# Adapter matmuls of a four-layer attention kernel in fp16 halves, transposed by DMA, and their layer-norm steps ahead of the score maxima

## The chip, the cores and the metric

The kernel runs on one core of a Trainium2 chip. The metric is the device time of one execution in microseconds, the median of three runs.

## The reference, cut to what matters

Eight batches, each with `x` and `f` of 512 tokens by 512. Four residual layers follow one another:

```python
x = x + L0(x, f)                       # 16-head attention, keys from x (masked by length) and one own key from f; then Wo
q = x + embed[stage]                   # L1
x = x + softmax(q @ f.T) @ f
h = relu(x @ W1[lang] + b1[lang])      # L2, the adapter: W1 512x128, W2 128x512
y = x + h @ W2[lang] + b2[lang]
x = x + layernorm(y) * gamma[lang] + beta[lang]
t = x @ lora_A[rl].T                   # L3, rank 16
x = x + t @ lora_B[rl].T + lang_embed[rl]
```

The change concerns L2 and L3. `lang` and `rl` are chosen per batch, so their weights are loaded for each batch.

## The kernel before, in words

All matrices of 128 partitions are handled by tiles of 128 tokens; a batch has four (`NT`), and 512 columns are four blocks of 128 (`ND`). Large products are made in fp16 with each operand as a high and a low half, by three matmuls a pair (`hi_lo`, L478): high by high, low by high, high by low. Halves are made by GpSimd (`split`, L513 and L515), by ScalarE and VectorE together, or by VectorE. Matrices `xT` and `fT` (tokens along the free axis) come from `split16` by a transposing DMA on SyncE's queue (`turn`, L698).

The program is unrolled over batches. Each engine runs the same list of steps in its own order: attention of batch i (scores, ScalarE's exponentials, values), then `layer1` (Wo and L1), then `mid`. `mid` is made of three interleaved things:

- the projections of the next batch i+1: `K`, `Q`, `KS`, `VS`, `V`, each cut into six parts of two matmuls. The prediction calls one such part a slot; there are 117 of them, numbered from 0, K of group 0 having 0 to 5, Q 6 to 11, KS 12 to 17, and so on by 18 for a group;
- 64 steps `SMAX` of the next batch (the maxima): TensorE makes a 128x512 score tile (L1378), VectorE takes its row maximum (L1095), ScalarE the exponential with its sum (L816). Two pairs of banks (4 and 6) hold four such tiles at a time. One `SMAX` follows each slot, in four groups of 16 that open at slots 35, 53, 71 and 89. `SMAX` of group g needs `KQ`, filled by 12 DMAs (L645) from the halves that GpSimd makes of Q and K (`HALF`);
- the adapter steps (L2 and L3) of batch i, one after every other slot, from the list `adapters` of `order_mid`. All use bank 2 on TensorE.

For one tile of 128 tokens the adapter steps before are: `X2T` (TensorE transposes x in fp32, L1280; ScalarE evicts it to `x2T`, L833; GpSimd adds b2, L550), `HID` (four fp32 matmuls of 128 columns, L1406; ScalarE relu, L839), `ADP` (one fp32 matmul of 512 columns, L1411; VectorE adds and sums, L1141), `SQ` (ScalarE, L845), `NORM` (for two tiles at a time: 15 small VectorE instructions in five pieces, L1035 to L1048, then two L1053; GpSimd adds beta, L556), `SCALE` (GpSimd times gamma, L560, and add, L563), `X3T` (fp32 transposes; VectorE copies, L1152), `LOW` (four fp32 matmuls with the rank-16 rows; ScalarE, L851), `LORA` (fp32 matmul of 512 columns, L1433; VectorE adds, L1156; SyncE stores).

After the last `SMAX` come `MROW` and `SROW`, which turn maxima and sums into the shift rows and normalisers that attention of the next batch needs. Batch 0 has a `mid` without adapters, and the last batch has the adapters without projections (`order_last`).

In attention, VectorE makes four copies of lora_B (L1193), and TensorE transposes the small tables (`small_tables`); ScalarE evicts them (L871).

## Times and profile before

| | us |
|---|---|
| median of 3 runs | 1296.07 (1295.64 to 1298.99) |
| the profiled execution | 1295.73 |
| its span | 1294.0 |
| TensorE busy | 1257.0 (97%) |
| VectorE busy | 864.2 (67%) |
| ScalarE busy | 847.8 (66%) |
| GpSimd busy | 490.0 (38%) |
| share of the last chain: TensorE, VectorE, ScalarE | 69%, 15%, 12% |

From the second batch on the kernel repeats with a period of 156.10 us: layer 1 of a batch, its `mid`, attention of the next. The period shown below begins at 598.80 us; the first row of the windows is its layer 1, the next three are `mid` (to the opening of the maxima, the maxima, the rest), the fifth is attention. A matmul's record lasts longer than the distance to the next, since matmuls overlap; what one costs TensorE's queue is read from the chain, whose pieces do not overlap.

### The profile page before, as it was taken

What the parts mean: (1) busy time and instruction counts of PE and PEld (TensorE: products, weight loads), DVE (VectorE), ACT (ScalarE), POOL (GpSimd) and SP (SyncE); (2) the same over time, 40 slices, a digit from 0 to 9 for tenths busy, and PEclk for the clock granted to TensorE, in tenths of its full rate; (3) what the DMA queues carried; (4) which work ended last, traced back from release to release, by engine and by line L of the source; (5) the groups of instructions that cost most, each with busy time, mean ns of one, the idle gap of its engine ahead of it and who ended that gap; (6) DMA issues with size and microseconds to landing.
All of it is one profiled execution on the core that took longest, in us unless ns stands there. A gap on an engine that the chain in (4) does not pass through costs nothing.

```text
span 1294.0 us, 19231 instructions
## 1 busy us (share of the span) xinstructions
PE 1257.0 (97%) x6697; PEld 523.5 (40%) x6697; DVE 864.2 (67%) x1561; ACT 847.8 (66%) x1795; POOL 490.0 (38%) x428
## 2 busy tenths in 40 slices
...
GB/s 217 83 6 107 124 57 66 79 80 99 52 63 122 37 98 68 47 125 63 86 58 50 117 79 77 58 50 108 98 75 66 46 95 124 50 66 90 4 33 33
DMA packets 156142, 98.85 MB, mean 76 GB/s; under 512 B 107338, under 2 KB 130182, under 8 KB 156046
## 3 DMA queue, kind: packets, MB, share of 16 engines
...
## 4 chain that ended last, share of the span: by engine, by line
PE 69%; DVE 15%; ACT 12%; issue 2%; POOL 1%; DMA 1%; SPq 0%; ACTq 0%; POOLq 0%; DVEq 0%
PE bank L478 25%; PE banks L478 13%; PE banks L1443 8%; DVE nmx L1095 8%; PE bank L1459 7%; ACT banks L816 5%; PE banks L1378 4%; ACT big L867 4%; PE bank L1280 3%; PE bank L1406 2%; PE bank L1411 2%; PE bank L1433 2%; PE bank L1469 1%; DVE y L1053 1%; ACT bank L896 1%
## 5 line engine op out<-in xcount | busy, mean ns | idle before, releaser
L816 ACT ACTIVATE banks<-banks,nmx 128x512 f32<-128x512 f32 x512 | 341.2, 682 | 40.2 <-DVE nmx L1095 37.8
L1095 DVE TENSOR_REDUCE nmx<-banks 128x1 f32<-128x512 f32 x512 | 329.2, 687 | 19.5 <-PE banks L1378 18.6
L867 ACT ACTIVATE big<-banks 128x1024 f32<-128x1024 f32 x256 | 248.0, 1021 | 54.4 <-PE banks L1443 53.4
L478 PE MATMUL bank<-fT,w_hi 128*128 128x512 f16 x768 | 255.7, 379 | 0.6 <-DVE fT L1009 0.6
L1378 PE MATMUL banks<-KQ 97*128 97x512 f16 x512 | 195.6, 382 | 8.1 <-ACT banks L816 7.9
L513 POOL TENSOR_TENSOR split<-tiles_in,ones 128x512 f16<-128x512 f32 x56 | 62.0, 1108 | 224.7 <-DMA xT<-split 205.7
L1443 PE MATMUL banks<-KQ 98*128 98x512 f16 x512 | 143.5, 383 | 3.6 <-DVE q L1116 0.2
L478 PE MATMUL bank<-fT,w_lo 128*128 128x512 f16 x384 | 145.4, 379 | 0.0
L513 POOL TENSOR_TENSOR half<-qk,ones 128x512 f16<-128x512 f32 x64 | 68.4, 1069 | 200.6 <-ACT qk L798 192.5
L1459 PE MATMUL bank<-big,V 128*32 128x512 f32 x1024 | 136.4, 605 | 0.0
L588 POOL TENSOR_TENSOR x<-x,bo_rows 128x512 f32<-128x512 f32 x32 | 39.9, 1275 | 206.5 <-DMA x<-in_x_dram 206.5
L816 ACT ACTIVATION_READ_ACCUMULATOR banks<-banks,nmx 128x1 f32 x512 | 116.5, 227 | 0.0
L478 PEld LDWEIGHTS bank<-fT,w_hi 128*128 128x128 f16 x768 | 75.1, 98 | 82.0 <-issue 12.8
L1378 PEld LDWEIGHTS banks<-KQ 97*128 97x128 f16 x512 | 49.1, 96 | 104.5 <-ACT banks L816 56.9
L478 PE MATMUL bank<-fT,q1T 128*128 128x512 f16 x384 | 88.2, 379 | 1.8 <-DVE q1T L1213 1.8
L1443 PEld LDWEIGHTS banks<-KQ 98*128 98x128 f16 x512 | 34.2, 97 | 129.3 <-ACT big L867 100.0
L478 PE MATMUL bank<-xT,w_hi 128*128 128x512 f16 x256 | 84.3, 381 | 0.5 <-ACT qk L798 0.5
L478 PE MATMUL banks<-split,p_both 128*128 128x512 f16 x384 | 84.5, 379 | 0.0
L478 PE MATMUL bank<-w_hi,xT 128*128 128x512 f16 x256 | 81.5, 379 | 0.0
L560 POOL TENSOR_TENSOR y<-y,gr 128x512 f32<-128x512 f32 x32 | 42.8, 1337 | 92.5 <-DVE y L1053 92.5
L515 POOL TENSOR_TENSOR half<-qk,half 128x512 f16<-128x512 f32 x64 | 75.5, 1179 | 5.0
L478 PE MATMUL banks<-w_hi,xT 128*128 128x512 f16 x256 | 76.3, 380 | 0.0
(154 smaller groups left out, 1822.0 us busy)
## 6 DMA issues: line engine op xcount, KB each, us to landing
...
```

The lines of the kernel that those rows point to most:

```text
L478: mm = eng.matmul(out_ap, pairs[n][0], pairs[n][1], start=(first and n == 0), stop=(last and n == len(pairs) - 1))
L513: eng.tensor_tensor(high, src, ones[:, 0:1].to_broadcast([P, S]), ALU.mult).then_inc(high_done, 1)
L515: eng.tensor_tensor(low, src, high, ALU.subtract).then_inc(low_done, 1)
L560: eng.tensor_tensor(y[:, t % 2, :], y[:, t % 2, :], gr[:, :], ALU.mult).then_inc(scaled, 1)
L588: eng.tensor_tensor(x1[:, t, :], x1[:, t, :], bo_rows[:, :], ALU.add).then_inc(x_bo, 1)
L816: eng.activation(bank(step, i)[:, v, :], bank(step, i)[:, v, :], ACT.Exp, bias=nmx[:, t, h:h + 1], accum_out=esum[:, t, h:h + 1]).then_inc ...
L867: eng.activation(big[:, n % 2, 2 * u:2 * u + 2, :], bank(step)[:, :, :], ACT.Exp).then_inc(read(step), 1)
L1095: eng.tensor_reduce(nmx[:, t, h:h + 1], bank(step, i)[:, v, :], AX_X, ALU.max, negate=True).then_inc(max_done, 1)
L1280: mm = eng.transpose(tile_of(step, b)[:, d * P:(d + 1) * P], src[:, d * P:(d + 1) * P], ident[:, :])
L1378: eng.matmul(bank(step, i)[:, v, :], KQ[0:SHIFT_ROW, j, g, 1, t * P:(t + 1) * P], KQ[0:SHIFT_ROW, j, g, 0, :], start=True, stop=True).then ...
L1443: mm = eng.matmul(bank(step)[:, j % 2, :], KQ[0:SHIFT_ROW + 1, j, g, 0, k * P:(k + 1) * P], KQ[0:SHIFT_ROW + 1, j, g, 1, :], start=True, s ...
L1459: mm = eng.matmul(bank(("PV", g))[q, :], V[:, k, g * P + j * DH:g * P + (j + 1) * DH], big[:, n % 2, j, :], start=(k == 0), stop=(k == NT ...
```

## The change: what it does

- `X2T` and `X3T` leave TensorE for the seven batches with a next one. x2 is split into halves by ScalarE (`X2`) and VectorE (within `PV1` of layer 1), x3 by GpSimd (`X3`); both are transposed by DMA into `aT2` (L736, four turns each, `T3` for x3). The first f turn now stands ahead of the last p1 turn in SyncE's queue, the other three behind it.
- `HID` and `LOW` work on 256 tokens (two steps instead of four) with fp16 halves: 12 matmuls and 8 matmuls of 256 columns. `LORA` is one fp16 matmul; `ADP` stays fp32. W1 is loaded into `hT` and split by GpSimd (three instructions a batch). VectorE makes the low rows of `LOW`.
- `NORM` is once for all four tiles, 11 small instructions instead of twice 15. `U` (centre, times gamma) and `SCALE` (times the inverse deviation, plus x) are one VectorE instruction each for a tile; GpSimd's two of `SCALE` go, and `L1053` too.
- `HID` to `SCALE` stand ahead of slot 35, where the maxima open; `X3` to `LORA` in the slots up to 74.
- lora_B is copied by one instruction, the small tables are evicted mostly by VectorE, and lang_embed comes by its own small DMA into `erow`. Two `memset` more at the start. The last batch keeps its transposes on TensorE, and splits what they give.

```diff
-        adapters = [("X2T", 0), None, ("HID", 0), None, ("ADP", 0), None, ("X2T", 1), ("SQ", 0), ("HID", 1), ("ADP", 1),
-                    ("SQ", 1), n0[0], ("X2T", 2), n0[1], ("HID", 2), n0[2], ("X2T", 3), n0[3], ("HID", 3), n0[4],
-                    n0[5], None, ("SCALE", 0), None, ("SCALE", 1), ("X3T", 0), None, ("LOW", 0), None, ("ADP", 2),
...
+        at = {3: [("HID", 0)], 5: [("ADP", 0)], 6: [("ADP", 1), ("SQ", 0), ("HID", 1)], 7: [("SQ", 1)], 8: [("U", 0), ("ADP", 2)],
+              9: [("ADP", 3), ("SQ", 2), ("U", 1)], 10: [("SQ", 3), ("U", 2)], 11: [("NORM", 0), ("U", 3)],
+              12: [("SCALE", 0), ("SCALE", 1)], 13: [("SCALE", 2), ("SCALE", 3)], 16: [("X3", 0)], 17: [("X3", 1)],
+              18: [("X3", 2)], 19: [("X3", 3), ("T3", 0), ("T3", 1)], 20: [("T3", 2), ("T3", 3)],
+              28: [("LOW", 0)], 30: [("LORA", 0)], 32: [("LORA", 1)], 33: [("LOW", 1)], 35: [("LORA", 2)], 37: [("LORA", 3)]}
...
-    out, later = [], {}
+    out, later = [("X2", t) for t in range(NT) if tail], {}
...
# GpSimd
+                        if head:
+                            eng.wait_ge(f_lo, (i + 1) * NT + t + 1)
                         wait_read(eng, ("PV1", t), i)
-                        eng.tensor_tensor(xb[:, t % 2, :], x1[:, t, :], b2r[:, :], ALU.add).then_inc(xb_done, 1)
+                        eng.tensor_tensor(yb[:, t, :], x1[:, t, :], b2r[:, :], ALU.add).then_inc(xb_done, 1)
+                        if head and t == NT - 1:
+                            add_beta(range(NT), head, i)
+                    elif step[0] == "X3":
+                        eng.wait_ge(x3_done, i * NT + t + 1)
+                        eng.wait_ge(x2t_in[t // 2], i * 32 + 32)
+                        split(p16[:, t, 0:S], p16[:, t, S:2 * S], x1[:, t, :], x3_hi, i * NT + t + 1, x3_lo)
-                        eng.tensor_tensor(y[:, t % 2, :], y[:, t % 2, :], gr[:, :], ALU.mult).then_inc(scaled, 1)
...
-                        eng.tensor_tensor(x1[:, t, :], y[:, t % 2, :], x1[:, t, :], ALU.add).then_inc(x3_done, 1)
+            def split_w1(i):
+                eng.wait_ge(w1_in, i * 16 + 16)
+                eng.tensor_tensor(hT[:, :], hT[:, :], wide[:, 0:1].to_broadcast([P, S]), ALU.mult).then_inc(w1_wide, 1)
+                eng.wait_ge(w1_wide, i + 1)
+                halves = w1[:].rearrange("p h d n -> p h (d n)")
+                split(halves[:, 0], halves[:, 1], hT[:, :], w1_hi, i + 1, w1_lo)
# SyncE
                 for t in range(NT):
+                    if head and t == NT - 1:
+                        wait_full(eng, ("S1", NT - 1), i)
+                        turn_f(0, b)
...
+                    for n in range(1, NT):
+                        turn_f(n, b)
+                    for t in range(NT):
+                        eng.wait_ge(x2_lo, i * NT + t + 1)
+                        turn(aT2, t, p16[:, t, :], x2t_in[t // 2])
# ScalarE
+                    elif kind == "X2":
+                        wait_read(eng, ("PV1", t), i)
+                        eng.activation(p16[:, t, 0:S], x1[:, t, :], ACT.Copy).then_inc(x2_hi, 1)
# VectorE
+                        if head:
+                            eng.wait_ge(x2_hi, i * NT + t + 1)
+                            eng.scalar_tensor_tensor(out=p16[:, t, S:2 * S], in0=x1[:, t, :], scalar=1.0, in1=p16[:, t, 0:S],
+                                                     op0=ALU.mult, op1=ALU.subtract).then_inc(x2_lo, 1)
+            def centre(t, i):
+                eng.wait_ge(sq_done, i * NT + t + 1)
+                eng.scalar_tensor_tensor(out=yb[:, t, :], in0=yb[:, t, :], scalar=st[:, t, 1:2], in1=gr[:, :],
+                                         op0=ALU.add, op1=ALU.mult).then_inc(normed, 1)
+            def scale(t, head, i):
+                eng.wait_ge(newton, (i + 1 if head else i + 1 + t // 2) * NEWTON)
...
+                eng.scalar_tensor_tensor(out=x1[:, t, :], in0=yb[:, t, :], scalar=st[:, t, 4:5], in1=x1[:, t, :],
+                                         op0=ALU.mult, op1=ALU.add).then_inc(x3_done, 1)
# TensorE
+                        if head:
+                            eng.wait_ge(x2t_in[step[1]], i * 32 + 32)
...
+                        hi_lo(eng, bank(step, i)[:, 0:at.stop - at.start], [(w1[:, 0, d, :], w1[:, 1, d, :]) for d in range(ND)],
+                              [(aT2[:, 0, d, at], aT2[:, 1, d, at]) for d in range(ND)]).then_inc(done(step, i), 1)
...
+                        for d in range(ND):
+                            for h in range(2):
+                                rows = a16[:, h, d, :, :].rearrange("p c r -> p (c r)")
+                                mm = eng.matmul(bank(step, i)[0:3 * LR, 0:at.stop - at.start], rows, aT2[:, h, d, at],
+                                                start=(d == h == 0), stop=(d == ND - 1 and h == 1))
```

On VectorE, around the opening of the maxima, the program before has small statistics instructions (L1044 and its like) between `KS` products (L1084) and the first maxima (L1095):

```order
L1042 TENSOR_TENSOR st<-st 128x2
L1084 SCALAR_TENSOR_TENSOR prod<-bank,bias_ks,qk 128x512
L1095 TENSOR_REDUCE nmx<-banks 128x1 x4
L1044 TENSOR_TENSOR st<-st 128x2
L1046 TENSOR_SCALAR st<-st 128x2
L1048 TENSOR_TENSOR st<-st 128x2
L1095 TENSOR_REDUCE nmx<-banks 128x1 x2
L1053 TENSOR_SCALAR y<-y,st 128x512 x2
L1095 TENSOR_REDUCE nmx<-banks 128x1 x10
```

In the changed program the same place reads as follows (L1092 is the last of the small instructions, L1097 is `U`, L1104 `SCALE`, L1135 the product, L1146 the maxima):

```order
L1190 SCALAR_TENSOR_TENSOR tiles_in,st<-bank,tiles_in 128x512
L1194 TENSOR_SCALAR st<-st 128x1
L1097 SCALAR_TENSOR_TENSOR tiles_in<-tiles_in,st,gr 128x512 x2
L1083 TENSOR_SCALAR st<-st 128x4
...
L1092 SCALAR_TENSOR_TENSOR st<-st 128x4
L1097 SCALAR_TENSOR_TENSOR tiles_in<-tiles_in,st,gr 128x512
L1104 SCALAR_TENSOR_TENSOR x<-tiles_in,st,x 128x512 x4
L1135 SCALAR_TENSOR_TENSOR prod<-bank,bias_ks,qk 128x512
L1146 TENSOR_REDUCE nmx<-banks 128x1 x16
```

The whole of the statistics, with four `SCALE`, now stands in front of the first maximum, and the 16 maxima of a group are together.

On TensorE the place from the start of `mid` reads before, with transposes (L1280), `HID` (L1406) and `ADP` (L1411):

```order
L1280 MATMUL bank<-ident,x 128x128 x4
L478 MATMUL bank<-xT,w_hi 128x512 x2
...
L1406 MATMUL bank<-big,w 128x128 x4
L478 MATMUL bank<-xT,w_lo 128x512
...
L1411 MATMUL bank<-w,hT 128x512
```

and after the change (L504 with `big,w` is `HID`, L1503 `ADP`):

```order
L504 MATMUL bank<-big,w 128x256 x12
...
L1503 MATMUL bank<-w,hT 128x512
L504 MATMUL bank<-fT,w_lo 128x512
L504 MATMUL bank<-fT,w_hi 128x512 x2
L504 MATMUL bank<-fT,w_lo 128x512
L1503 MATMUL bank<-w,hT 128x512
L504 MATMUL bank<-big,w 128x256 x12
```

The second `HID` stands right behind the second `ADP`, in the same bank.

On SyncE's queue the part from the xT turns to the mask row was:

```order
L698 DMA_TRANSPOSE xT<-split 128x8x128 x4
L712 DMA_TRANSPOSE p_both<-big 128x8x128 x4
L698 DMA_TRANSPOSE fT<-split 128x8x128 x4
L636 DMA KQ<-mask_rows 1x16x512
L645 DMA KQ<-half 32x2x512 x4
```

and is now, with the four turns of x2 behind those of f:

```order
L736 DMA_TRANSPOSE xT<-split 128x8x128 x4
L756 DMA_TRANSPOSE p_both<-big 128x8x128 x3
L736 DMA_TRANSPOSE fT<-split 128x8x128
L756 DMA_TRANSPOSE p_both<-big 128x8x128
L736 DMA_TRANSPOSE fT<-split 128x8x128 x3
L736 DMA_TRANSPOSE big<-big 128x8x128 x4
L674 DMA KQ<-mask_rows 1x16x512
L683 DMA KQ<-half 32x2x512 x4
```

## Rows read from the trace of the kernel before

**Rows 1.** Windows: length, busy of PE, PEld, DVE, ACT, POOL; clock, DMA, GB/s

```profile
598.80:630.20 31.40, 31.18 (x154) 15.04 (x153) 16.12 (x31) 10.04 (x20) 9.88 (x9) 1.00 0.63 124
630.20:652.10 21.90, 21.90 (x124) 12.54 (x123) 7.91 (x20) 7.75 (x15) 13.86 (x13) 1.00 0.23 49
652.10:708.40 56.30, 55.52 (x289) 24.08 (x287) 51.83 (x102) 51.16 (x146) 22.49 (x19) 1.00 0.23 56
708.40:715.40 7.00, 7.00 (x41) 3.37 (x41) 4.41 (x8) 3.73 (x8) 0.00 (x0) 1.00 0.11 37
715.40:754.90 39.50, 39.13 (x226) 9.31 (x224) 25.52 (x29) 31.68 (x34) 14.69 (x12) 1.00 0.31 91
...
1223.20:1294.00 70.80, 55.76 (x265) 29.18 (x263) 32.74 (x86) 18.34 (x40) 20.49 (x16) 0.83 0.13 30
```

**Rows 2.** Chain that ended last, from 637 us: start, length, engine, tile, line

```profile
638.00 0.44 PE bank L1280 x4
638.43 1.73 PE bank L478 x8
640.16 0.89 PE bank L1406 x8
...
667.04 0.35 PE bank L1424 x8
...
670.11 0.86 PE bank L1411 x2
...
677.48 0.86 PE bank L1433 x2
```

**Rows 3.** ScalarE's exponentials in `mid`: source line in batch 0, then the period

```profile
L816 ACT ACTIVATE banks<-banks,nmx x64: 650/728/925, 37.6 to 85.1; 128x512 f32<-128x512 f32 x64
...
L816 ACT ACTIVATE banks<-banks,nmx x64: 650/664/738, 653.7 to 708.7; 128x512 f32<-128x512 f32 x64
```

**Rows 4.** TensorE timeline: first score matmuls of attention, steady, then batch 0

```profile
715.28 1.03 PE L1443 MATMUL banks<-KQ 98*128 98x512 f16 x4
717.44 1.13 PE L1443 MATMUL banks<-KQ 98*128 98x512 f16 x4
...
92.10 1.03 PE L1443 MATMUL banks<-KQ 98*128 98x512 f16 x4
```

**Rows 5.** Groups by line, 630 to 716 us: evictions

```profile
L798 ACT ACTIVATE qk<-bank,bias_k 128x512 f32<-128x512 f32 x4 | 2.8, 695 | 0.4 <-PE bank L478 0.4
...
L851 ACT ACTIVATE lowT<-bank,ident 128x128 f32<-128x128 f32 x4 | 1.5, 372 | 0.2 <-PE bank L1424 0.2
```

**Rows 6.** Timeline of VectorE and GpSimd where both work from SBUF

```profile
569.17 5.01 POOL L588 TENSOR_TENSOR x<-x,bo_rows 128x512 f32<-128x512 f32 x4 [24.47 <-DMA x<-in_x_dram]
...
569.57 3.43 DVE L1193 COPY smallb<-smallb 128x64 f32<-128x64 f32 x4 [3.52 <-DMA smallb<-in_L_cond_lora_B_dram]
...
645.59 0.17 DVE L1046 TENSOR_SCALAR st<-st 128x2 f32<-128x2 f32 x1
645.79 1.00 DVE L1048 TENSOR_TENSOR st<-st 128x2 f32<-128x2 f32 x1
...
649.49 0.16 DVE L1042 TENSOR_TENSOR st<-st 128x2 f32<-128x2 f32 x1
...
645.73 1.04 POOL L513 TENSOR_TENSOR half<-qk,ones 128x512 f16<-128x512 f32 x1 [1.42 <-ACT qk L798]
```

**Rows 7.** VectorE's two-input instruction from SBUF: source line, whole run

```profile
L1180 DVE SCALAR_TENSOR_TENSOR xT<-y,cols,xT x32: 750/752/1603, 110.1 to 1225.3; 128x512 f16<-128x512 f32 x32
```

**Rows 8.** SyncE's queue: issue times by source, landing time by issue group

```profile
L698 SPq DMA_TRANSPOSE fT<-split x4: 1323/1332/1337, 624.7 to 628.8; - x4
...
fT<-split SPq DMA_TRANSPOSE x28, 3.3
```

**Rows 9.** Timeline of the last batch's end, GpSimd

```profile
1279.34 1.50 POOL L560 TENSOR_TENSOR y<-y,gr 128x512 f32<-128x512 f32 x1 [5.91 <-DVE y L1053]
1280.91 1.26 POOL L563 TENSOR_TENSOR x<-y,x 128x512 f32<-128x512 f32 x1
```

More of the change, by code:

```diff
@@ L122, in order_mid @@
         if adapters and i % 2 == 0:
-            out += [a for a in (adapters.pop(0),) if a]
+            out += adapters.pop(0)
         if rows and not sums and i >= late and not adapters:
@@ L134, in order_mid @@
     assert rows and i >= max(later)
-    return out + [a for a in adapters if a] + ([] if sums else [("SROW",)])
+    return out + [a for each in adapters for a in each] + ([] if sums else [("SROW",)])
 OPEN = ((32, 26, 26, 26), (24, 24, 24, 24))
@@ L598, in _ @@
             add_bo(B - 1)
-            mid(True, False, B - 1, [step for step in order_last() if step in ADAPTER_STEPS])
+            split_w1(B - 1)
+            mid(True, False, B - 1, [step for step in order_last() if step[0] in ADAPTERS])
         @block.sync
```

353 lines of the change are left out of this document (198 added, 155 removed).

## The prediction, made before the changed kernel was run

> **What bounds the kernel now.** I read the windows of one period first [rows 1]. TensorE is busy for 31.18 of 31.40 us in layer 1, for all of the 21.90 us before the maxima, for 55.52 of 56.30 in the maxima and for 39.13 of 39.50 in attention: as a queue it bounds every stage. But in the maxima ScalarE has 51.16 busy us and VectorE 51.83 in 56.30, so they stand close behind. Second, the chain of waits, whose pieces on TensorE give what a step costs its queue [rows 2]. Third, the exponentials of the maxima, since batch 0 has the same `mid` without adapters and so shows what is left when TensorE has less to do [rows 3]. Last, the places where VectorE and GpSimd both work from SBUF [rows 6, 7].
>
> The profiled execution took 1295.73 us, with 1.7 outside its span of 1294.0, and stands 0.3 under the median of 1296.07. The sum is made against 1295.73. Seven batches have a `mid` with adapters; what is worked out for one period counts seven times.
>
> **TensorE's part.** By the chain, a tile's turn costs 0.44 us, `HID` 0.89, `ADP` 0.86, `LOW` 0.35, `LORA` 0.86, and an fp16 matmul of 512 columns 1.73 / 8 = 0.216 [rows 2]. Before, one period has 8 turns (3.5), 4 `HID` (3.6), 4 `ADP` (3.4), 4 `LOW` (1.4) and 4 `LORA` (3.4): 15.3 us. After, it has 24 matmuls of 256 columns in `HID`, 16 in `LOW`, 4 of 512 in `LORA` and the same `ADP`. No row shows an fp16 matmul of 256 columns. The nearest is a record of `HID`, 0.89 / 8 = 0.111 us; the upper bound is a matmul of 512 columns, 0.216. At 0.111: 2.7 + 1.8 + 0.9 + 3.4 = 8.8 us, which saves 6.5. At 0.216 it saves 2.4. I take 0.111. If TensorE stayed the bound, the change would be worth 6.5 x 7 = 46 us.
>
> **It doesn't stay the bound in the maxima.** In batch 0 the 64 exponentials start between 37.6 and 85.1 us; with 0.66 for the last, ScalarE needs 48.2 us for them with what lies between, and it hardly waits there. In the period they take from 653.7 to 709.4, 55.7 us [rows 3]. After the change ScalarE has what it has in batch 0, and one more eviction of K (0.70) and two of `LOW` (0.37 each, rows of 128 columns; 256 may take 0.5) [rows 5]: 49.8 us from the first exponential to the end of the last. TensorE's queue needs less: 64 x 0.216, 70 slots of 0.43, three `SELF`, `LOW` and `LORA` make about 47.6. So ScalarE sets this stage, and it counts from its first exponential, not from TensorE's arrival.
>
> What follows the last exponential is also read in batch 0: it ends at 85.8, and the second block of attention's scores starts at 92.10; in the period that block stands 717.44 - 715.28 = 2.16 behind the first, so attention begins in effect at 89.9, which is 4.1 after the last exponential [rows 4]. Attention of the next batch then begins at T + 49.8 + 4.1, where T is the first exponential. Before, it begins at 715.28, with T at 653.7. The gain of a period is therefore 715.3 - 53.9 - T = 661.4 - T. Everything hangs on T.
>
> **T: the statistics in front of the first maximum.** All on the time axis of this period, whose `mid` begins at 630.2 [rows 1].
> TensorE: the second `HID` stands right behind the second `ADP` in the same bank, so it waits for VectorE's eviction, 0.9 us. To the end of the fourth `ADP` there are 19 slots (8.2), two `HID` (2.7), four `ADP` (3.4) and that wait: 645.4. To slot 35 come 17 slots and a `SELF`: 653.1, against 652.1 before. So the opening itself moves by 1 us.
> VectorE: it evicts the fourth `ADP` by 646.3, ScalarE's square takes 0.9, two `U` fill the wait until about 647.8. Then 11 small instructions at 645.79 - 645.59 = 0.20 (2.2), the last `U` and four `SCALE` at 0.75 each (3.8; the nearest row is L1180, also two inputs from SBUF, at least 0.750) [rows 6, 7], the product (0.75) and the first maximum (0.69). Alone that gives T = 655.3.
> It is not alone. While GpSimd runs, VectorE's instructions from SBUF wait: four copies that take 0.18 alone took 3.43 us under GpSimd's four instructions of 5.01, and five small ones from 645.79 to 649.49 took 3.7 us where 1.0 is their own time; L1180 goes up to 1.603 [rows 6, 7]. GpSimd splits K and Q of group 1 at about 648.2 to 650.4 and 650.8 to 653.0 (1.04 for the first of a pair [rows 6], the second a little more), right over the small instructions: +2.7, as in the row. Its splits of x3 begin as soon as the first `SCALE` is done and run against the other three: half an instruction each, +1.2. I take T = 659.2, with 655.3 at one end. At the other end each of the last `U` and the four `SCALE` waits for a whole GpSimd instruction of 1.1: 655.3 + 2.7 + 5.5 = 663.5.
> The Trainium skill states this rule: "GPSIMD Engine Reference", section 1 Specifications, says that GpSimd's SBUF interfaces are shared with VectorE and contended by VectorE instructions with two SBUF inputs or in a two-port mode. It speaks against this change, since `U`, `SCALE` and the low half of x2 have two SBUF inputs, where the maxima and evictions from PSUM have not. By that rule the trace agrees, with the 3.43 us of the four copies beside it. Without the rule T would be 655.3.
>
> At T = 659.2 the gain is 2.2 us a period, 15.5 in seven.
>
> **Turns and queues.** SyncE issues the f turns in 1.33 each and they land 3.3 after their issue [rows 8]. The first f turn now goes before the last p1 turn, behind which the f turns began at 624.7 before; the other three then end at 628.7, and the first two of x2 are issued by 631.3 and land at 633.3. `HID` stands at 633.2: no stall. The low half of x2's last tile is done at about 634.7 (VectorE waits on GpSimd's f splits), it lands at 638.0, and the second `HID` asks at 640.2. Behind these turns wait the mask row and the stack of group 0; GpSimd's adds of b2 and beta, eight at 5.01 / 4 = 1.25 [rows 6], all stand before `HALF` of K 0 now, five more than before, of which some three fall beyond its former idle time: Q 0's halves and the stack come about 4 us later. TensorE had no idle time before the opening [rows 1], so the stack was in time there; it may now be 0.6 late for TensorE, and that is hidden, as VectorE comes only at 658. The x3 turns end before the stack of group 2 is wanted. I cost all of this at nothing; were VectorE early, the 0.6 would show.
> Layer 1: the four extra VectorE instructions fall into its waits for `PV1`, and GpSimd's three for W1 into its long wait for the xT turns: nothing.
> **Attention.** One copy for four of lora_B, and small tables on VectorE, which has 25.52 busy us in 39.50 [rows 1]: nothing in the period, and in batch 0, where the chain goes over those copies, 0.7 gained.
> **The last batch.** Here the adapters are serial, in 70.80 us with the granted clock at 0.83, between its levels of 1.2 and 2.4 GHz [rows 1]. Each pair of tiles loses GpSimd's 1.50 + 1.26 [rows 9] for one `SCALE` of 0.75 (twice -2.0) and four small instructions (twice -0.8); `LORA` in fp16 saves some 0.6 twice; each turn needs a second eviction of 0.65 behind the first, three or four times on the chain (+2.3), and `LOW` a low row (+0.4). I take -4, between -8 (no second eviction on the chain) and +3 (all on it, and nothing gained by `SCALE`).
>
> **Sum.** 1295.7 - 15.5 - 0.7 - 4 = 1275.5; I say 1275 us.
>
> **The rivals.**
> *VectorE is early.* If contention costs little, T = 655.3 to 656 and a period gains 6; 1295.7 - 6 x 7 - 4.7 = 1249 us. For it: GpSimd has gaps in that stage (13.86 busy of 21.90 [rows 1]), and its splits might be the ones that wait. Against it: rows 6. It is also nearly the time if TensorE stayed the bound (46 + 4.7: 1245).
> *The second end: slower.* The same queue on VectorE decides from T = 661.4 on; each us beyond costs 7. At T = 663.5, when every `U` and `SCALE` pays a GpSimd instruction, a period loses 2.1: 1295.7 + 14.7 - 4.7 = 1306 us. For it: L1180's 1.603, twice its own time. Against it: GpSimd has no work between Q 1's halves and x3's, so the fourth `U` and first `SCALE` run free.
> *The turns are late.* If eight turns in a row do not land 3.3 after their issue but 2 us later, `HID` stalls TensorE and shifts the statistics with it: 14 us of the gain go, about 1290 us. For it: the landing time was never seen with more than four turns behind each other. Against it: DMA engines are 0.23 to 0.63 busy there [rows 1].
> *Nothing changes.* The delay of VectorE takes just what TensorE gives: within 4 us of before, about 1294.
>
> **Chances and range.** A measurement of this kernel tells 0.3% (3.9 us) from no change. Forecast (1262 to 1285) 0.50; early VectorE 0.25; late turns 0.10, mostly still faster; nothing changed 0.06; slower 0.09. The range that holds 8 in 10 leaves out the end of both outer cases: 1246 to 1292. Faster by over 0.3% 0.84, within 0.3% 0.07, slower by over 0.3% 0.09.
>
> **What would show it.** In the profile after: the first exponential of a period 28 or 29 us behind the start of `mid` (T) and 64 of them in 50 us with hardly a wait; small statistics instructions of about 1 us where GpSimd runs; TensorE idle 4 to 5 us a period behind its first four maxima, released by ScalarE or VectorE; a 256-column matmul every 0.11 us; no wait of `HID` for a DMA; TensorE's busy share down, the period at about 153.9 us. Wrong I would be if TensorE had no gap at the opening (VectorE early), if `HID` waited for its turns, or if the exponentials had gaps inside their 50 us.

## The result and the profile after

The changed kernel takes 1328.1 us (median of 4 runs, 1327.1 to 1329.05) against 1296.1 us before: a ratio of 1.0237 with a 95% interval of 1.0217 to 1.0257, 32.0 us slower where 20 us faster were forecast. The profiled execution has a span of 1325.3 us, 31.3 more than before.

These are the windows of one period after the change, cut at the same places as [rows 1] and in the same columns: layer 1, what stands before the first score matmul of the maxima, from there to the first exponential, the exponentials, what lies behind them, attention; and the last batch.

```profile
core 0: us, PE busy (x) PEld busy (x) DVE busy (x) ACT busy (x) POOL busy (x), PEclk, DMA share, GB/s
934.53:965.76 31.23, 31.00 (x152) 14.88 (x152) 19.20 (x35) 11.93 (x23) 12.18 (x11) 1.00 0.59 101
965.76:990.01 24.25, 22.75 (x113) 10.65 (x112) 14.88 (x31) 7.33 (x15) 16.50 (x14) 1.00 0.39 78
990.01:996.40 6.39, 2.78 (x13) 1.07 (x11) 6.39 (x8) 0.00 (x1) 4.95 (x5) 1.00 0.37 83
996.40:1051.00 54.60, 50.04 (x244) 20.28 (x245) 45.29 (x72) 49.73 (x143) 13.87 (x13) 0.97 0.31 73
1051.00:1055.30 4.30, 4.30 (x23) 2.09 (x22) 3.00 (x6) 2.34 (x4) 0.00 (x0) 1.00 0.01 4
1055.30:1094.73 39.43, 39.18 (x227) 9.63 (x226) 23.32 (x31) 31.50 (x33) 17.86 (x15) 1.00 0.38 116
1255.29:1325.30 70.01, 50.72 (x275) 28.37 (x275) 40.12 (x91) 20.06 (x44) 10.45 (x8) 0.83 0.12 31
```

Layer 1 and attention are what they were (31.23 and 39.43 against 31.40 and 39.50). The last batch is 0.8 us shorter. The whole loss lies in the seven `mid`, around one event: for 6.39 us ScalarE does nothing and VectorE is busy without a pause, and TensorE works for 2.78 of them. Then ScalarE needs 54.60 us for its 64 exponentials, though it is busy for 49.73.

Three stretches of a period carry the comparison below; they are means over the seven periods of each profiled execution: (a) from the start of attention to the next first exponential, (b) the 64 exponentials, (c) from their end to the start of the next attention. The start of attention is taken 2.16 us ahead of its second block of scores, as the prediction does with [rows 4]. "Waits" are ScalarE's waits for VectorE's maxima within (b); its waits for TensorE, which come in where `LOW` is late, are not in that column.

| kernel | a | b | c | period | waits |
|---|---|---|---|---|---|
| before | 94.7 | 55.7 | 5.9 | 156.2 | 3.1 |
| after | 101.5 | 54.8 | 4.6 | 160.9 | 4.9 |

(a) grew by 6.8 us, (b) and (c) gave 0.9 and 1.3 back: 4.6 us a period, 32.5 in seven, less 1.1 in the last batch's attention and adapters. (b) is 54.5 to 54.6 in five of the periods after the change and 55.9 and 55.2 in the other two.

**The opening.** VectorE's queue ahead of the first maximum (timeline: start, duration, engine, line, operation, names, shapes):

```profile
985.17 0.17 DVE L1090 SCALAR_TENSOR_TENSOR st<-st 128x4 f32<-128x4 f32 x1
985.37 1.04 DVE L1092 SCALAR_TENSOR_TENSOR st<-st 128x4 f32<-128x4 f32 x1
986.45 0.17 DVE L1088 SCALAR_TENSOR_TENSOR st<-st 128x4 f32<-128x4 f32 x1
986.65 1.01 DVE L1090 SCALAR_TENSOR_TENSOR st<-st 128x4 f32<-128x4 f32 x1
989.12 1.65 DVE L1097 SCALAR_TENSOR_TENSOR tiles_in<-tiles_in,st,gr 128x512 f32<-128x512 f32 x1
990.70 4.41 DVE L1104 SCALAR_TENSOR_TENSOR x<-tiles_in,st,x 128x512 f32<-128x512 f32 x4
995.03 0.74 DVE L1135 SCALAR_TENSOR_TENSOR prod<-bank,bias_ks,qk 128x512 f32<-128x512 f32 x1
995.69 1.87 DVE L1146 TENSOR_REDUCE nmx<-banks 128x1 f32<-128x512 f32 x3
```

GpSimd in the same stretch, splits of K and Q of group 1 and then of x3:

```profile
985.35 1.04 POOL L541 TENSOR_TENSOR half<-qk,ones 128x512 f16<-128x512 f32 x1 [5.77 <-ACT qk L846]
986.47 1.17 POOL L543 TENSOR_TENSOR half<-qk,half 128x512 f16<-128x512 f32 x1
991.51 1.48 POOL L541 TENSOR_TENSOR big<-x,ones 128x512 f16<-128x512 f32 x1 [1.29 <-DVE x L1104]
```

The small instruction at 985.37 begins 0.02 behind GpSimd's and ends with it, at 986.4, though 0.17 is its own time; the one at 986.65 ends with the second split. Three of the eleven are stretched so, the third (0.91 at 988.10) by the next split. The last `U` (989.12) takes 1.65 in place of 0.75 beside a fourth. The four `SCALE` (L1104) take 4.41 us and run against the splits of x3, which themselves take 1.48 in place of 1.04: the very work that the first `SCALE` releases slows those behind it. T is 996.40, which is 61.87 behind the start of layer 1, or 660.7 on the axis of the prediction.

**TensorE in the opening** (three rows of its timeline, the wait ahead of each in brackets), and windows over its clock:

```profile
969.56 1.47 PE L504 MATMUL bank<-big,w 128*128 128x256 f16 x12 [0.61 <-DMA big<-big]
976.42 1.47 PE L504 MATMUL bank<-big,w 128*128 128x256 f16 x12 [0.89 <-DVE tiles_in L1190]
997.23 0.39 PE L1466 MATMUL banks<-KQ 97*128 97x512 f16 x1 [4.44 <-ACT banks L864]
```

```profile
994.00:996.00 2.00, 0.00 (x0) 0.00 (x0) 2.00 (x3) 0.00 (x0) 2.00 (x2) 1.00 0.46 106
998.00:999.00 1.00, 1.00 (x4) 0.33 (x3) 1.00 (x3) 1.00 (x4) 0.92 (x2) 0.50 0.58 121
1002.00:1003.00 1.00, 1.00 (x6) 0.45 (x5) 1.00 (x2) 0.94 (x3) 0.92 (x2) 1.00 1.09 203
```

Behind 4.44 idle us the granted clock is at its lower level of 1.2 GHz (0.50), here from 997.9 to 1001.3. Every period has such a stretch at its opening; it lasts 3.4 us in five of them and 6.8 in the two with the longer (b).

**The exponentials.** ScalarE's rows within the maxima that have a wait ahead of them, and the last one; then two of VectorE's:

```profile
996.40 0.66 ACT L864 ACTIVATE banks<-banks,nmx 128x512 f32<-128x512 f32 x1 [8.53 <-DVE nmx L1146]
1009.64 0.66 ACT L864 ACTIVATE banks<-banks,nmx 128x512 f32<-128x512 f32 x1 [0.93 <-DVE nmx L1146]
1013.88 0.66 ACT L864 ACTIVATE banks<-banks,nmx 128x512 f32<-128x512 f32 x1 [1.21 <-DVE nmx L1146]
1023.27 0.66 ACT L864 ACTIVATE banks<-banks,nmx 128x512 f32<-128x512 f32 x1 [1.21 <-DVE nmx L1146]
1025.85 0.66 ACT L864 ACTIVATE banks<-banks,nmx 128x512 f32<-128x512 f32 x1 [1.13 <-DVE nmx L1146]
1028.84 0.66 ACT L864 ACTIVATE banks<-banks,nmx 128x512 f32<-128x512 f32 x1 [0.21 <-DVE nmx L1146]
1050.25 0.73 ACT L864 ACTIVATE banks<-banks,nmx 128x512 f32<-128x512 f32 x1
```

```profile
1008.25 0.75 DVE L1135 SCALAR_TENSOR_TENSOR prod<-bank,bias_ks,qk 128x512 f32<-128x512 f32 x1 [0.60 <-PE bank L504]
1012.71 0.42 DVE L1211 SCALAR_TENSOR_TENSOR lowT<-bank,lowT 32x256 f16<-32x256 f32 x1 [1.31 <-ACT lowT L905]
```

Five gaps of 0.93 + 1.21 + 1.21 + 1.13 + 0.21 = 4.69 us. With them 49.8 becomes 54.5. At 1012.71 VectorE waits for ScalarE's eviction of `LOW`, which stands behind exponentials in ScalarE's queue, and right after it (1013.88) ScalarE waits for the maxima that VectorE has not taken meanwhile: a hand-off in order, paid on both sides.

**The last batch.** Its chain of waits shows the second evictions of a turn and the `SCALE` that GpSimd had in [rows 9]:

```profile
1305.47 0.61 ACT big L885
1306.10 0.70 DVE big L1206
1313.01 0.67 DVE x L1104
```

### The profile page after: what moved, and what is told of

It is laid out like the page before. It is cut to its first block, busy times and chain, and to the rows that moved or that the text cites. A ratio compares the mean times of both kernels' runs of the same rounds, so it can differ in the third digit from the quotient of the medians.

```text
span 1325.3 us, 18385 instructions
## 1 busy us (share of the span) xinstructions
PE 1221.2 (92%) x6289; PEld 483.9 (37%) x6289; DVE 920.6 (69%) x1500; ACT 838.8 (63%) x1763; POOL 513.4 (39%) x445
## 4 chain that ended last, share of the span: by engine, by line
PE 45%; ACT 26%; DVE 20%; issue 4%; DMA 3%; SPq 1%; POOL 0%; ACTq 0%; DVEq 0%; POOLq 0%
ACT banks L864 17%; PE bank L504 14%; PE banks L504 8%; PE banks L1538 8%; PE bank L1554 7%; DVE nmx L1146 4%; PE bank L1503 2%; DVE x L1104 2%; ACT big L920 2%; PE banks L1466 2%; DVE tiles_in L1097 2%; ACT bank L947 2%; DMA big<-big 2%; DVE nmax L1304 1%; DVE st L1090 1%
## 5 line engine op out<-in xcount | busy, mean ns | idle before, releaser
L1146 DVE TENSOR_REDUCE nmx<-banks 128x1 f32<-128x512 f32 x512 | 329.9, 687 | 40.8 <-PE banks L1466 39.0
L504 PE MATMUL bank<-fT,w_hi 128*128 128x512 f16 x768 | 256.7, 383 | 0.6 <-DVE fT L1062 0.6
L1466 PE MATMUL banks<-KQ 97*128 97x512 f16 x512 | 202.3, 395 | 53.5 <-ACT banks L864 51.8
L504 PE MATMUL bank<-fT,w_lo 128*128 128x512 f16 x384 | 147.1, 383 | 0.0
L541 POOL TENSOR_TENSOR half<-qk,ones 128x512 f16<-128x512 f32 x64 | 71.7, 1120 | 150.7 <-ACT qk L846 140.3
L864 ACT ACTIVATION_READ_ACCUMULATOR banks<-banks,nmx 128x1 f32 x512 | 122.7, 240 | 0.0
L504 PEld LDWEIGHTS bank<-fT,w_hi 128*128 128x128 f16 x768 | 76.1, 99 | 82.9 <-issue 12.1
L504 PE MATMUL bank<-fT,q1T 128*128 128x512 f16 x384 | 88.2, 380 | 1.8 <-DVE q1T L1297 1.8
L504 PE MATMUL bank<-xT,w_hi 128*128 128x512 f16 x256 | 87.6, 394 | 0.1
L504 PE MATMUL banks<-split,p_both 128*128 128x512 f16 x384 | 84.7, 379 | 0.2 <-DMA p_both<-big 0.2
L504 PE MATMUL bank<-w_hi,xT 128*128 128x512 f16 x256 | 80.3, 379 | 0.0
L504 PE MATMUL banks<-w_hi,xT 128*128 128x512 f16 x256 | 76.4, 380 | 0.0
L582 POOL TENSOR_TENSOR tiles_in<-x,b2r 128x512 f32<-128x512 f32 x32 | 41.3, 1295 | 76.9 <-DVE x L1072 76.9
```

The lines of the kernel that those rows point to most:

```text
L504: mm = eng.matmul(out_ap, pairs[n][0], pairs[n][1], start=(first and n == 0), stop=(last and n == len(pairs) - 1))
L541: eng.tensor_tensor(high, src, ones[:, 0:1].to_broadcast([P, S]), ALU.mult).then_inc(high_done, 1)
L582: eng.tensor_tensor(yb[:, t, :], x1[:, t, :], b2r[:, :], ALU.add).then_inc(xb_done, 1)
L864: eng.activation(bank(step, i)[:, v, :], bank(step, i)[:, v, :], ACT.Exp, bias=nmx[:, t, h:h + 1], accum_out=esum[:, t, h:h + 1]).then_inc ...
L1146: eng.tensor_reduce(nmx[:, t, h:h + 1], bank(step, i)[:, v, :], AX_X, ALU.max, negate=True).then_inc(max_done, 1)
L1466: eng.matmul(bank(step, i)[:, v, :], KQ[0:SHIFT_ROW, j, g, 1, t * P:(t + 1) * P], KQ[0:SHIFT_ROW, j, g, 0, :], start=True, stop=True).then ...
```

## The experiments

All are edits of the changed kernel. (a), (b), (c) and the waits of all of them, in us as above:

| kernel | time | a | b | c | waits |
|---|---|---|---|---|---|
| after | 1328.1 | 101.5 | 54.8 | 4.6 | 4.9 |
| e1 later opening | 1332.7 | 105.2 | 53.6 | 2.8 | 4.0 |
| e2 no low row | 1315.6 | 101.3 | 53.3 | 4.6 | 3.3 |
| e3 x3 splits late | 1343.4 | 99.8 | 58.6 | 4.5 | 5.9 |
| e4 LORA late | 1339.4 | 101.5 | 54.2 | 7.0 | 4.4 |
| e5 two halves | 1344.7 | 103.4 | 55.1 | 4.6 | 5.1 |
| e6 low row lags | 1324.2 | 101.6 | 54.2 | 4.5 | 4.0 |
| e7 two Newton steps | 1323.0 | 100.9 | 54.6 | 4.6 | 4.8 |
| e8 SCALE within | 1329.7 | 97.1 | 59.4 | 4.6 | 7.0 |
| e9 spread | 1290.6 | 97.3 | 53.9 | 4.5 | 2.9 |
| e10 spread, two steps | 1284.1 | 96.5 | 53.8 | 4.6 | 2.8 |
| e11 TensorE kept busy | 1319.5 | 101.6 | 53.6 | 4.6 | 4.0 |
| e12 spread, LOW later | 1273.2 | 96.7 | 52.0 | 4.6 | 1.3 |
| e13 statistics within | 1287.3 | 96.7 | 54.1 | 4.5 | 3.2 |

**The idle time and the clock: e11 and e1.** First TensorE kept busy in its gap:

```
+ if tail and (g, u, v) == (0, 2, 0):
+     wait_read(eng, ("ADP", 3), i)
+     for _ in range(20):
+         eng.matmul(bank(("ADP", 3), i)[:, :], KQ[0:SHIFT_ROW, 0, 0, 1, 0:P], KQ[0:SHIFT_ROW, 0, 0, 0, :], ...)
```

> The changed kernel with twenty needless matmuls of 512 columns (4.3 us, into the adapters' free bank) in TensorE's 4.4 us of idle time behind the first four score matmuls; nothing else is moved. Theory A (the fall of the granted clock behind the idle time costs the exponentials only the gap of 0.93 us): the clock stays at its upper level, 7 x 0.9 = 6 us, 1322. Rival B (the clock falls all the same, or the idle time has nothing to do with it): 1328. Rival C (the slow stretch costs its 3.4 us at half rate, 1.7 to 3.4 us a period): 1304 to 1316.

Measured 1319.5 us (ratio to before 1.0173, 1.0156 to 1.0190), 8.7 less. A window where the slow stretch was (2 us behind the first exponential of its period), and ScalarE's first two waits in another period:

```profile
992.00:994.00 2.00, 2.00 (x10) 0.64 (x9) 2.00 (x5) 2.00 (x7) 1.92 (x3) 1.00 0.70 137
```

```profile
830.94 0.66 ACT L864 ACTIVATE banks<-banks,nmx 128x512 f32<-128x512 f32 x1 [8.54 <-DVE nmx L1146]
843.20 0.66 ACT L864 ACTIVATE banks<-banks,nmx 128x512 f32<-128x512 f32 x1 [0.29 <-DVE nmx L1146]
```

The clock stays at 1.00, T is where it was, the gap of 0.93 shrinks to 0.29, and the exponentials take 53.64 in every period, in place of 54.6 in five and of 55.9 and 55.2 in the two periods whose slow stretch was twice as long. The measured 1319.5 lies between A's 1322 and C's 1316, nearer to A. A's mechanism holds, with 0.9 us for a stretch of 3.4; what A left out is the two longer stretches, which make it 1.2 us a period in the mean, 8.5 in seven.

The other way to fill the gap, the first maxima ten slots later:

```
-OPEN = ((32, 26, 26, 26), (24, 24, 24, 24))
+OPEN = ((32, 26, 26, 26), (34, 24, 24, 24))
```

> The changed kernel with its first maxima of the period ten slots of projection later in TensorE's order (45 instead of 35), nothing else. Reference point: the changed kernel at 1328.1 us; in its trace every period has TensorE idle for 4.4 us behind the first four score matmuls, then 3.4 us at a granted clock of 0.50, and the exponentials wait 8.5 us ahead of the first and 4.7 us in five gaps behind it. Theory A (the gaps are a sum of separate causes, each worth its own wait): the idle time and the slow clock go, and with them only the gap of 0.93 us at the 13th microsecond, which came from TensorE's debt; 7 x 0.9 = 6 us, 1322, T (first exponential) the same 61.9 us behind the start of layer 1. Rival B (the slow clock is the main cause of the loss): 7 x 3.4 = 24 us, 1304. Rival C (the order behind is worse: the last maxima stand 4 slots nearer to attention): 7 x 1 = 7 us slower, 1335.

Measured 1332.7 (1.0283, 1.0266 to 1.0300): slower, but not for rival C's reason, since (c) fell by 1.7. TensorE is stopped before it comes to slot 45:

```profile
999.45 0.39 PE L504 MATMUL bank<-fT,w_hi 128*128 128x512 f16 x1 [3.05 <-DVE prod L1135]
```

It waits for the bank that `prod` of group 1 reads, and `prod` stands behind `SCALE` in VectorE's queue. T is 3.7 later, and the clock falls again behind this gap (0.50 from 999.8 to 1003.2). All three expectations missed: VectorE's queue holds TensorE by a second string.

**LOW's hand-off: e2 and e6.**

```
- at = tokens(step, head)
- eng.wait_ge(low_hi, ...)
- eng.scalar_tensor_tensor(out=lowT[LR:2 * LR, at], ...)
+ pass        # and ScalarE's eviction frees the bank
```

This leaves out the low part of the low-rank product, so it prices the work and is no way to run the kernel.

> The changed kernel without VectorE's low row in LOW (the subtraction that makes the second half of the low-rank product); ScalarE's eviction alone frees the bank. It leaves out the low part of the low-rank product. Theory A (the hand-off from ScalarE's eviction to VectorE inside the maxima costs, since both queues are in order: VectorE waited 1.31 and 1.55 us for it, and ScalarE 1.21 twice for the maxima behind): 7 x 2.4 = 17 us, 1311, with the waits of exponentials behind LOW gone. Rival B (ScalarE is behind anyway and takes the gaps elsewhere, as VectorE's total work is the bound): within 4 us of 1328. Rival C (T alone counts): 1328.

Measured 1315.6 (1.0161, 1.0144 to 1.0178): 12.5 us, three quarters of what A expected; B and C fall. Then the same work, placed later in VectorE's queue:

```
- 28: [("LOW", 0)], 30: [("LORA", 0)], 32: [("LORA", 1)], 33: [("LOW", 1)], 35: [("LORA", 2)], 37: [("LORA", 3)]
+ 28: [("LOW", 0)], 29: [("ROW", 0)], 31: [("LORA", 0)], 32: [("LORA", 1)], 33: [("LOW", 1)], 34: [("ROW", 1)], 36: [("LORA", 2)], 37: [("LORA", 3)]
```

> The changed kernel with VectorE's low row of LOW two maxima behind ScalarE's eviction in its queue, not right behind it; the first and third LORA two slots later, for the bank. Nothing is left out. Theory A (what costs is the hand-off in order, VectorE waiting for ScalarE and then ScalarE for VectorE): as without the low row at all, which gave 12.5 us, so 1315 to 1316, and no wait of VectorE at the low row. Rival B (the work itself costs, 2 x 0.42 us of VectorE): 1325 to 1328.

Measured 1324.2 (1.0214, 1.0197 to 1.0231), 4 us: just outside B's range, and far from A's 1315 to 1316. VectorE no longer waits at the low row:

```profile
1011.20 0.42 DVE L1212 SCALAR_TENSOR_TENSOR lowT<-bank,lowT 32x256 f16<-32x256 f32 x1
```

but low rows and `LORA` still follow each other with two to four maxima between them, and a gap returns among them:

```profile
861.60 0.66 ACT L864 ACTIVATE banks<-banks,nmx 128x512 f32<-128x512 f32 x1 [1.16 <-DVE nmx L1146]
```

So moving the hand-off alone does not bring what e2 brought. The rows fit a crowd, in which the gap that one piece no longer makes comes up at the next; that is a reading of them and has no run of its own.

**LORA behind the maxima: e4.**

```
+ 53: [("LORA", 0)], 54: [("LORA", 1)], 55: [("LORA", 2)], 56: [("LORA", 3)]
```

> The changed kernel with its four LORA steps behind the last maximum instead of between the maxima (slots 106 to 112), LOW where it was. Theory A: VectorE is freed of 4 x 0.69 us within the maxima, the gap of 1.13 us and the one of 0.21 us go: 7 x 1.3 = 9 us, 1319. Rival B (the row sums and norms wait for LORA and its stores now, and attention for them): 7 x 1.5 = 10 us slower, 1338. Rival C (VectorE's work within the maxima is the bound of the stage): 7 x 2.8 = 19 us faster, 1309.

Measured 1339.4 (1.0337, 1.0319 to 1.0354), 11 us slower, by rival B's figure. (b) gained 0.7, (c) lost 2.4. What the rows show is more than B's wait of attention: the four `LORA` share one bank, their evictions stand behind the steps of the row sums in VectorE's queue, and TensorE, which is busy for all of (c) in the change as it is, waits for each of them.

```profile
898.48 0.39 PE L1528 MATMUL bank<-lowB,lowT 97*128 97x512 f16 x1 [1.17 <-DVE x L1217]
```

**The queue ahead of T: e3, e5, e7, e8.** x3's splits moved behind the halves of K 2 and Q 2:

```
- 16: [("X3", 0)], 17: [("X3", 1)], 18: [("X3", 2)], 19: [("X3", 3), ("T3", 0), ("T3", 1)], 20: [("T3", 2), ("T3", 3)],
+ 22: [("X3", 0), ("X3", 1), ("T3", 0), ("T3", 1)], 25: [("X3", 2), ("X3", 3), ("T3", 2), ("T3", 3)],
```

> The changed kernel with GpSimd's splits of x3 (and their turns) behind the halves of K 2 and Q 2 in its queue, so that none of them runs beside the four SCALE. Theory A (contention with GpSimd stretches SCALE to 4.41 us where 4 x 0.70 + 0.1 = 2.9 is their own, and that stands in T): T falls by 1.5 us, and the period with it, 7 x 1.5 = 10 us, 1318. Rival B (contention has little to do with it, SCALE takes 1.1 each by itself): 1328. Rival C (the halves of K 2 and Q 2, or the x3 turns, are late for their maxima or for LOW instead): 1335.

Measured 1343.4 (1.0361, 1.0341 to 1.0381). Both halves of the argument are in its rows, from VectorE and from TensorE:

```profile
836.96 2.73 DVE L1104 SCALAR_TENSOR_TENSOR x<-tiles_in,st,x 128x512 f32<-128x512 f32 x4
```

```profile
855.63 1.07 PE L1522 MATMUL bank<-big,a 128*96 128x256 f16 x8 [0.65 <-DMA big<-big]
868.47 1.94 PE L1522 MATMUL bank<-big,a 128*96 128x256 f16 x8 [4.22 <-DMA big<-big]
```

Without GpSimd beside them the four `SCALE` take 2.73 in place of 4.41, and (a) falls by just that, 1.7: A's mechanism is shown. But the turns of x3 are now late for `LOW`, TensorE stands for 4.22 us, the granted clock falls there too (0.50 from 866.4 to 873.3), and (b) loses 3.8: rival C decides the time.

Statistics in two halves:

```
- 8: [("U", 0), ("ADP", 2)], 9: [("ADP", 3), ("SQ", 2), ("U", 1)], ... 11: [("NORM", 0), ("U", 3)], 12: [("SCALE", 0), ("SCALE", 1)],
+ 8: [("U", 0), ("U", 1), ("NORM", 0), ("ADP", 2)], 9: [("ADP", 3), ("SQ", 2)],
+ 10: [("SQ", 3), ("U", 2), ("SCALE", 0), ("SCALE", 1)], 11: [("U", 3), ("NORM", 1)],
```

> The changed kernel with the statistics in two halves, those of tiles 0 and 1 in VectorE's idle time before the third adapter eviction, and two of the four SCALE ahead of the second half; eleven more small instructions in all. Theory A (T, the first exponential, is set by VectorE's queue, and each us of T is a us of the period): T falls by 2 us (1 to 3), 7 x 2 = 14 us, 1314 (1307 to 1321). Rival B (what is taken from T comes back as waits within the maxima, VectorE's total being the bound): within 4 us of 1328. Rival C (eleven more small instructions meet GpSimd and cost more than they save): 1335.

Measured 1344.7 (1.0391, 1.0366 to 1.0416): rival C, and more than it said. The first eleven take 0.16 each with GpSimd idle; of the second eleven seven are stretched. One row of each:

```profile
990.13 0.16 DVE L1088 SCALAR_TENSOR_TENSOR st<-st 128x2 f32<-128x2 f32 x1
998.42 1.00 DVE L1088 SCALAR_TENSOR_TENSOR st<-st 128x2 f32<-128x2 f32 x1
```

```profile
998.24 1.17 POOL L543 TENSOR_TENSOR half<-qk,half 128x512 f16<-128x512 f32 x1
```

Of the seven the first four meet GpSimd's splits of K and Q and the other three those of x3, which the early `SCALE` have released and which follow without a gap. One Newton step less:

```
-NEWTON = 11
+NEWTON = 8
```

> The changed kernel with two instead of three Newton steps for the inverse square root, three small instructions fewer a period (8 instead of 11). Theory A (T, set by VectorE's queue under GpSimd's splits, moves the period one to one): own time 3 x 0.2 = 0.6 us, and one of the three waits of 0.85 for GpSimd gone: T falls by 0.6 to 1.5 us, 7 x that = 4 to 10 us, 1318 to 1324. Rival B (what T loses comes back as waits of the exponentials): within 3 us of 1328.

Measured 1323.0 (1.0209, 1.0192 to 1.0226), 5 us, in A's range, though T is not all of it: (a) is 0.5 less, a little under A's 0.6, which makes 3.8 in seven; (b) is 0.3 less; and the last batch, whose two rounds of small instructions lose a step too, is 1.0 shorter, which A had not counted. `SCALE` within the maxima:

```
- 12: [("SCALE", 0), ("SCALE", 1)], 13: [("SCALE", 2), ("SCALE", 3)], 16: [("X3", 0)], ...
+ 18: [("SCALE", 0)], 20: [("SCALE", 1)], 22: [("SCALE", 2), ("X3", 0), ("X3", 1), ("T3", 0), ("T3", 1)],
+ 24: [("SCALE", 3)], 25: [("X3", 2), ("X3", 3), ("T3", 2), ("T3", 3)],
```

> The changed kernel with the four SCALE between the maxima of the first group (slots 36, 40, 44, 48) instead of ahead of the first maximum, the splits of x3 behind the halves of K 2 and Q 2. Theory A (VectorE's queue ahead of the first maximum is what the change pays for): T falls by 4.4 to 5 us; VectorE's own work within the maxima becomes 47.0 + 3.0 = 50.0 us and so equal to ScalarE's 49.8, so that half of it comes back as waits: a period gains 2 to 3 us, 1307 to 1314; TensorE's idle 4.4 us and the slow clock behind them go as well. Rival B (each SCALE within the maxima costs a whole gap of 0.75 or more, as LORA did): 4 x 0.75 + lost hiding = 1325 to 1330. Rival C (T is the whole story): 7 x 5 = 35 us, 1293.

Measured 1329.7 (1.0265, 1.0236 to 1.0293), in B's range. (a) fell by 4.3, near A's 4.4, (b) rose by 4.5. Two causes in its rows, from ScalarE and TensorE: gaps at the `SCALE`, though not B's 0.75 at each (0.41 at the first, none at the second, 0.86 and 0.31 at the others, which take 1.54 and 1.36 beside GpSimd in place of 0.74), and turns late for `LOW` again.

```profile
836.28 0.66 ACT L864 ACTIVATE banks<-banks,nmx 128x512 f32<-128x512 f32 x1 [0.41 <-DVE nmx L1146]
```

```profile
863.08 1.07 PE L1522 MATMUL bank<-big,a 128*96 128x256 f16 x8 [2.57 <-DMA big<-big]
```

**The spread: e9, e10, e12, e13.** Each VectorE instruction beside an eviction that ScalarE has in the maxima:

```
+ 20: [("SCALE", 0)], 21: [("X3", 0)], 22: [("T3", 0)], 23: [("SCALE", 1)], 24: [("X3", 1)], 25: [("T3", 1)],
+ 29: [("SCALE", 2)], 30: [("X3", 2)], 31: [("T3", 2)], 32: [("SCALE", 3)], 33: [("X3", 3)], 34: [("T3", 3)],
+ 35: [("LOW", 0)], 36: [("ROW", 0)], 38: [("LORA", 0)], 41: [("LORA", 1)], 42: [("LOW", 1)], 43: [("ROW", 1)],
+ 44: [("LORA", 2)], 47: [("LORA", 3)]
```

> The changed kernel with SCALE, LOW and LORA spread over the whole of the maxima, each beside an eviction that ScalarE has there (SCALE at the evictions of K 2, Q 2, K 3 and Q 3, LORA at those of V's rows), the x3 splits one by one behind the halves of K and Q in GpSimd's queue, the low row two maxima behind the eviction, so that no x3 turn is late for LOW. Theory A (the loss is a sum: T, and a wait of the exponentials for every VectorE instruction that no ScalarE instruction pays for): T 4.3 us earlier as measured with SCALE within the maxima, exponentials in 51 to 53 us instead of 54.5: a period gains 6 to 8 us, 1272 to 1286. Rival B (every instruction of VectorE within the maxima costs its gap wherever it stands): 54.5 + 2 = 56.5 us of exponentials, a period gains 2.3: 1312. Rival C (T3 turns, or GpSimd in one row with both tasks, are late again): 1300 to 1330.

Measured 1290.6 (0.9941, 0.9919 to 0.9963): 37.5 us below the changed kernel and below the one before, though 5 above A's range. (a) is 4.2 less, (b) 0.9 less. e10, with two Newton steps:

> The spread of e9_match with two Newton steps instead of three. Theory A: as the same edit gave alone (5 us), 5 us below e9_match. Rival B: nothing, if the opening of e9_match isn't set by VectorE any more but by TensorE's arrival.

Measured 1284.1 (0.9907, 0.9887 to 0.9927), 6.5 less: A's figure, but rival B's limit is already there. From the first small instruction to the product VectorE has 6.1 us of work in e9 and 4.0 in e10, and (a) fell by 0.8 only, since VectorE now waits 1.7 us for TensorE ahead of the product. The last batch is 1.5 shorter as well. What e9 lacks of A's range fits a wait of its TensorE, again for an x3 turn, which e12 takes away:

```profile
836.25 1.07 PE L1524 MATMUL bank<-big,a 128*96 128x256 f16 x8 [1.45 <-DMA big<-big]
```

e12 takes e10 and moves `LOW` 0 from place 35 to 38 and what follows with it (`LOW` 1 to 44, the last `LORA` to 49):

> The spread with two Newton steps (1284.1 us) and LOW, its low row and LORA three slots of the pairs later, so that the x3 turns have landed when TensorE comes to LOW. In the trace of the spread with three steps TensorE waited 1.45 us for an x3 turn at the first LOW of a period and ScalarE 0.94 and 1.44 behind it. Theory A: that wait goes and 1 to 1.5 us a period with it, 7 to 10 us, 1274 to 1277. Rival B (LORA late and in the last slots collides with the end of the maxima and the stores with the row sums, as in e4_loralate): 1290 or more. Rival C (these waits only moved, since VectorE is as full as ScalarE): within 3 us of 1284.

Measured 1273.2 (0.9818, 0.9794 to 0.9841): 10.9 less than e10, a little more than A. The first exponential, and the next wait for a maximum; none of the four left in a period is over 0.38, and beside them ScalarE waits 0.75 for TensorE at an eviction of `LOW`:

```profile
799.74 0.66 ACT L865 ACTIVATE banks<-banks,nmx 128x512 f32<-128x512 f32 x1 [3.73 <-DVE nmx L1147]
812.02 0.66 ACT L865 ACTIVATE banks<-banks,nmx 128x512 f32<-128x512 f32 x1 [0.26 <-DVE nmx L1147]
```

The window of those exponentials, in the columns of the first table:

```profile
799.74:851.76 52.02, 48.88 (x249) 21.05 (x248) 47.77 (x76) 49.90 (x143) 17.96 (x16) 1.00 0.37 87
```

VectorE has more work within these exponentials than in the changed kernel (47.77 us against 45.29, the four `SCALE` included), and ScalarE waits less for it. So the gaps do not come from VectorE's amount of work alone: where it stands counts, beside the clock (1.00 here) and the turns of x3 (none late here).

e13 takes e12 and moves the last `U` and the small instructions behind the first maximum:

```
- 11: [("NORM", 0), ("U", 3)],
+ 18: [("U", 3), ("NORM", 0)],
```

> As e12_lowlater8, and the last centring (U 3) and the small instructions of the statistics moved behind the first maximum, where GpSimd is idle (between the halves of Q 1 and of K 2). Theory A (what still delays T is VectorE's queue under GpSimd's splits: 1.66 for U 3 and three waits of 0.85 in the small instructions): T falls by 4 us against the spread, the same instructions cost 2.4 us within the maxima, all of 0.17 to 0.2 each and none stretched: 1 to 1.5 us a period, 7 to 10 us below e12_lowlater8. Rival B (VectorE within the maxima is full: all that T loses comes back): the same as e12_lowlater8, within 3 us.

Measured 1287.3 (0.9930, 0.9906 to 0.9954), 14 us slower than e12: both theories missed. VectorE's product ahead of the first maximum in e12, then e13's with one of the small instructions:

```profile
798.36 0.75 DVE L1136 SCALAR_TENSOR_TENSOR prod<-bank,bias_ks,qk 128x512 f32<-128x512 f32 x1 [1.69 <-PE bank L505]
```

```profile
806.94 0.75 DVE L1136 SCALAR_TENSOR_TENSOR prod<-bank,bias_ks,qk 128x512 f32<-128x512 f32 x1 [5.58 <-PE bank L505]
809.87 0.17 DVE L1089 SCALAR_TENSOR_TENSOR st<-st 128x4 f32<-128x4 f32 x1
```

In e12, as in e10, VectorE already waits 1.69 us for TensorE ahead of `prod`: T is TensorE's arrival, and the small instructions, stretched or not, fill idle time. In e13 they run unstretched as expected (0.17), T does not move (96.7), and all of them show in (b), 2.1 longer. The wait in e12 stood in its trace before e13 was thought of as a theory of T; I took T for VectorE's without reading who waited.

## Why the prediction was wrong

**The failed step** is "49.8 us from the first exponential to the end of the last", with "hardly a wait". ScalarE's work was sized right: it is busy for 49.73. But the count was of ScalarE alone. The prediction saw that VectorE stood close behind ScalarE in the maxima of before (51.83 and 51.16 in [rows 1]) and then counted VectorE only ahead of the first maximum. It still has 45.3 us of work there, in an order where a low row waits for ScalarE and four `LORA` crowd together, and such places gave gaps: 4.7 us in the period shown, 4.9 in the mean. Batch 0, from which the 48.2 was taken, could not show them: VectorE has none of the adapters' work there, 42.5 us in 48.25, and ScalarE waits 0.2. e2, e6 and e11 each take a part of the gaps away, e9 and e12 most of them, down to 1.3 a period. It was the forecast's own sign of being wrong that came true: gaps inside the exponentials.

With 54.6 and 4.5 in place of 49.8 and 4.1 the gain of a period is 715.3 - 59.1 - T = 656.2 - T, not 661.4 - T. So the kernel is slower from T = 656.2 on, which the forecast's own T of 659.2 had passed. Of the 6.7 us between the 2.2 gained by forecast and the 4.5 lost in this period, 4.8 are the exponentials, 0.4 what follows them and 1.5 T. The rival on the slower side had the direction and not the step: it asked for T beyond 661.4, which was not reached.

**T** was mis-sized by 1.5: 660.7 for 659.2, within 655.3 to 663.5. Contention over the small instructions was as said (three stretched by 0.74 to 0.87, 2.5 for 2.7), and the x3 splits cost 1.7 over the four `SCALE` (e3) for 1.2; the fourth `U`, which was to run free, paid 0.9 beside GpSimd's split at 989.06; and the statistics began 1.0 later than said (984.56, or 648.8 on the prediction's axis, for 647.8), behind TensorE. The four `SCALE` alone take 2.73 where 3.0 was said. By the rule of the Trainium skill that the prediction cites, the trace agrees. The stretched rows end with GpSimd's instruction to 0.03 us; the Trainium skill, "SBUF — State Buffer", section SBUF: two separate sides, calls the shared pair an exclusive lock held for a whole instruction, and the 1.04 beside 0.17 has that form. The maxima, from PSUM, keep their 0.69 beside GpSimd.

**TensorE.** Sizes right: `HID` 1.31 for 12 matmuls (0.109 each; 0.111 said), the wait of the second `HID` 0.89 for 0.9. The opening comes 2.2 us later, not 1: of the 1.2 too much 0.61 is the wait of the first `HID` for its turn, where "no stall" was said. The idle time at the opening is 4.4, as foreseen (4 to 5). Its consequence was not: the granted clock falls behind it, which costs 0.9 us in most periods and 1.2 in the mean by e11.

**Turns.** Late by 0.6 at the first `HID`, a second of the forecast's signs of being wrong; nothing at the second. The x3 turns were in time in the change as it is, and late in e3, e8 and e9, which moved them.

**Nothing in layer 1 and attention**: right, 31.23 and 39.43. **Batch 0**: the (a) that holds its attention stood 0.6 above the others before and is level with them now, for the 0.7 said. **The last batch**: -0.8 for -4, within its range; the second evictions are all on the chain there (0.61 + 0.70 for a turn that had one of 0.70), and its small instructions, eleven twice, stand on it too.

**Not settled**: how much of e6's missing 8 us is the lag, how much the crowd of `LORA`; and whether the order of before would gain from the same spread with its own fp32 adapters, which was not run. So the 24 us by which e12 is below the kernel before, measured side by side (1273.2 and 1296.9), belong to the change with another order and one Newton step less, not to either alone.
